# Nine chunks of an RWKV layer on one core: new hand-written orders for all five engines

## What is computed

```
xn = ln(x, ln1);  sx = token_shift(xn)              # previous token minus this one
xxx = tanh((xn + sx*maa_x) @ maa_w1)                # five small mixes
x5 = xn + sx * (maa_stack + xxx @ maa_w2)           # five mixed inputs: k, w, v, r, g
w = exp(-exp(time_decay + tanh(x5[1] @ decay_w1) @ decay_w2))
r, k, v = x5[3] @ Wr.T, x5[0] @ Wk.T, x5[2] @ Wv.T;  g = silu(x5[4] @ Wg.T)
state s (8x8 per head, 32 heads), for each token t:
    a = k_t (x) v_t;  out_t = r_t . (u*a + s);  s = a + w_t * s
x = x + (groupnorm(out) * g) @ Wo.T
xn2 = ln(x, ln2); xr, xk = two mixes of xn2 and its token shift
x = x + sigmoid(xr @ ffn_Wr.T) * (relu(xk @ ffn_Wk.T)**2 @ ffn_Wv.T)
```

## Time and profile before

| | |
|---|---|
| runs | 520.23, 521.76, 522.25 us |
| profiled execution, first to last instruction | 520.3 us |
| VectorE busy | 474.4 us (91%), 528 instructions |
| TensorE busy | 479.2 us (92%) |
| ScalarE busy | 281.7 us (54%) |
| GpSimd busy | 101.6 us (20%) |
| DMA | 69.49 MB, mean 134 GB/s |

### The profile page before, as it was taken

The page is one execution under the profiler, slowest core; times in us unless marked ns, Lnnn a source line. Parts: engine busy times, 40 slices in busy tenths (PEclk is TensorE's granted clock), DMA queues, the critical chain, the costliest instruction groups (busy, mean ns, idle before and its releaser), DMA issues. The chain is left out here.

```text
span 520.3 us, 6254 instructions
## 1 busy us (share of the span) xinstructions
PE 479.2 (92%) x2200; PEld 284.2 (55%) x2200; DVE 474.4 (91%) x528; ACT 281.7 (54%) x612; POOL 101.6 (20%) x93
## 2 busy tenths in 40 slices
...
GB/s 265 121 231 52 107 166 85 145 217 151 72 204 230 122 26 167 220 217 19 103 219 242 85 81 139 216 201 1 121 189 220 78 61 227 126 72 71 1 41 30
DMA packets 26999, 69.49 MB, mean 134 GB/s; under 512 B 1624, under 2 KB 19928, under 8 KB 24536
## 3 DMA queue, kind: packets, MB, share of 16 engines
...
HBM read 46.28 MB, written 12.19 MB: 112 GB/s over the span
## 5 line engine op out<-in xcount | busy, mean ns | idle before, releaser
L630 DVE TENSOR_TENSOR_SCAN kv<-w_sb,kv 128x512 f32<-128x512 f32 (+2 forms) x144 | 146.6, 1084 | 0.1
L958 PE MATMUL pa<-x,large_sb 128*128 128x512 f32 (+2 forms) x272 | 115.2, 567 | 5.0 <-DVE x L545 2.9
L451 POOL COPY kv<-s_sb 128x32 f32<-128x32 f32 (+2 forms) x36 | 54.6, 1518 | 145.6 <-PE patt L1130 141.4
L958 PEld LDWEIGHTS pa<-x,large_sb 128*128 128x128 f32 x272 | 51.2, 194 | 57.5 <-issue 44.3
L620 DVE TENSOR_TENSOR kv<-vrep,k_sb 128x2016 f32<-128x2016 f32 (+2 forms) x34 | 70.1, 2064 | 3.3 <-issue 3.3
L638 DVE TENSOR_TENSOR kv<-kv,r_sb 128x2048 f32<-128x2048 f32 (+2 forms) x36 | 72.9, 2043 | 0.2
L536 DVE SCALAR_TENSOR_TENSOR x<-pb,vec_sb,sx 128x512 f32<-128x512 f32 (+1 forms) x64 | 42.7, 708 | 6.0 <-PE pb L1002 5.9
L420 POOL DMA_DIRECT2D x<-xn x21 | 20.0, 951 | 111.5 <-DVE x L536 111.5
L1130 PE MATMUL patt<-kv,const_sb 128*32 128x512 f32 (+2 forms) x288 | 34.7, 557 | 0.5 <-DVE kv L638 0.4
L1002 PE MATMUL pb<-th,w_sb 32*128 32x512 f32 (+2 forms) x100 | 33.3, 596 | 1.5 <-DVE x L536 1.5
L1156 PE MATMUL pc<-large_sb,att 128*128 128x256 f32 x120 | 32.0, 390 | 0.0
...
## 6 DMA issues: line engine op xcount, KB each, us to landing
...
x<-xn POOLq DMA_DIRECT2D x18, 512.0 KB, 8.3
...
x_tok<-in_x SPq DMA_DIRECT2D x6, 512.0 KB, 10.2
...
xres<-in_x SPq DMA_DIRECT2D x6, 512.0 KB, 10.7
out<-xres SPq DMA_DIRECT2D x6, 512.0 KB, 5.0
out<-trr POOLq DMA_DIRECT2D x6, 512.0 KB, 8.1
```

What stands on the lines that cost most here:

```text
L451: pool.tensor_copy(kv[:, q % 2, :, 0:nb, 0], s0_sb[:, half, G4 * j:G4 * (j + 1), FIRST[c]:FIRST[c] + nb]).then_inc(s0_put, 1)
L630: ins = dve.tensor_tensor_scan(flat, w_sb[:, p, q % HF, 0:nb].rearrange("p b t -> p (b t)"), flat, 0.0, ALU.mult, ALU.add)
L958: ins = pe.matmul(dst[:, m, 0:n], w(a)[:, m * P:(m + 1) * P], src[:, a, :], start=(a == 0), stop=(a == HF - 1))
```

## The change

The lists of head, table and tail are replaced by one list of steps for each engine, over all nine chunks. Every step of before is there once, none is added; instructions, buffers, transfers and `WARM` are the same. One wait is added: `vl1` now waits for the stored v itself, as `vl0` does, since in chunk 0 it comes first.

```
-def schedule(head, table, tail):
+def schedule(text):
+    return [(name, int(c)) for name, c in (step.split(".") for step in text.split())]
...
             def load_v(c, p, half):
-                if half == 0:
-                    sp.wait_ge(v_stored, 16 * JH * (c + 1))
+                sp.wait_ge(v_stored, 16 * JH * (c + 1))
```

The orders, before (-, as the lists unfold) and after (+), in the stretches that are spoken of below. VectorE, start, around `gate` of chunks 3 and 4, and end:

```
-st1.0 nrm1.0 shift.0 mix2.0 mix0.0 cwv.0 mix1.0 mix3.0 cs0.0 a0.0 a1.0 rk.0 shift.1 mix4.0 bonus.0 sc0.0 sc1.0 rs0.0 rs1.0
- mix0.1 a2.0 mix1.1 mix2.1 mix3.1 sc2.0 mix4.1 rs2.0 a3.0 sc3.0 rs3.0 rk.1 a0.1 shift.2 bonus.1 sc0.1 gate.0 mix0.2
+st1.0 nrm1.0 shift.0 cwv.0 mix0.0 mix2.0 mix1.0 mix3.0 cs0.0 a0.0 a1.0 sc0.0 mix4.0 shift.1 rk.0 rs0.0 sc1.0
+ bonus.0 mix0.1 mix1.1 rs1.0 a2.0 mix2.1 sc2.0 mix3.1 rs2.0 a3.0 mix4.1 sc3.0 rs3.0 rk.1 a0.1 bonus.1 shift.2 sc0.1 gate.0 a1.1 mix0.2
...
-rk.3 out.1 a0.3 shift.4 bonus.3 sc0.3 gate.2 rs0.3 mix0.4 mix1.4 a1.3 mix2.4 sc1.3 mix3.4 rs1.3 a2.3
+rk.3 out.1 a0.3 bonus.3 shift.4 a1.3 gate.2 mix0.4 mix1.4 sc0.3 mix2.4 sc1.3 mix3.4 rs0.3 rs1.3 shift2.2 a2.3
-rk.4 out.2 a0.4 shift.5 bonus.4 sc0.4 gate.3 rs0.4 mix0.5
+rk.4 out.2 a0.4 shift.5 bonus.4 gate.3 sc0.4 mix0.5 mix1.5 rs0.4
...
-sc2.7 a3.7 mix4.8 sc3.7 rs2.7 rs3.7 rk.8 out.6 a0.8 a1.8 bonus.8 gate.7 sc0.8 rs0.8 sc1.8 a2.8 sc2.8 rs1.8 rs2.8 shift2.7 a3.8 sc3.8 rs3.8 gate.8 out.7
+a3.7 sc2.7 sc3.7 rs2.7 rs3.7 mix4.8 out.6 a0.8 rk.8 a1.8 gate.7 bonus.8 sc0.8 rs0.8 sc1.8 rs1.8 a2.8 sc2.8 shift2.7 a3.8 sc3.8 rs2.8 rs3.8 out.7 gate.8
```

TensorE, start and end:

```
-T1.0 W1.0 X01.0 X2.0 X3.0 D1.0 D2.0 P0.0 P1.0 VS.0 P3.0 T1.1 CB.0 X4.0 P4.0 BO.0 W1.1 X01.1 S0.0 S1.0 P0.1
+T1.0 W1.0 X01.0 X2.0 X3.0 P0.0 D1.0 P1.0 VS.0 D2.0 T1.1 X4.0 P3.0 P4.0 W1.1 CB.0 X01.1 BO.0 S0.0 P0.1
...
-S2.7 S3.7 CB.8 VR.7 P4.8 WO.7 BO.8 S0.8 T2.7 S1.8 RR.7 S2.8 KK.7 S3.8 VR.8 Y2.7 WO.8
+S2.7 S3.7 VR.7 D2.8 P4.8 CB.8 WO.7 BO.8 S0.8 T2.7 S1.8 RR.7 KK.7 S2.8 S3.8 VR.8 Y2.7 WO.8
```

ScalarE, start and end; SyncE, start and chunk 4:

```
-st.0 nrm.0 xn.0 th.0 thd.0 st.1 v.0 w.0 nrm.1 k.0 r.0 xn.1 tg.0 th.1
+nrm.0 xn.0 st.0 th.0 st.1 thd.0 v.0 k.0 nrm.1 w.0 xn.1 r.0 tg.0 th.1
...
-rr.7 sq.8 kk.7 rstd.8
+rr.7 kk.7 sq.8 rstd.8
-vst.0 lx.0 lr.0 lx.1 lx.2 lx.3 vl0.0 vl1.0 vst.1 vl0.1 vl1.1 sx2.0 lx.4 vst.2 lr.1 vl0.2 vl1.2
+lx.0 lr.0 vst.0 lx.1 vl1.0 vl0.0 lx.2 vst.1 lx.3 vl0.1 vl1.1 sx2.0 vst.2 vl0.2 vl1.2 lr.1 lx.4
...
-vst.4 lr.3 lx.6 vl0.4 vl1.4
+vst.4 sx2.2 vl0.4 lx.6 lx.7 lr.3 vl1.4
```

More of the change, by code:

```diff
@@ L32 @@
 NQ = JH * HF
[L35 to L46, removed]
-SUBS = 3
[L48 to L64, removed]
[6 rows of a table removed]
-            ("out", 0), ("shift", 3), ("bonus", 2), ("sc0", 2), ("gate", 1), ("rs0", 2), ("mix0", 3),
-            ("mix1", 3)]
@@ L73 @@
-PE_HEAD = [("T1", 0), ("W1", 0), ("X01", 0), ("X2", 0), ("X3", 0), ("D1", 0), ("D2", 0), ("P0", 0), ("P1", 0),
[6 rows of a table removed]
-ACT_HEAD = [("st", 0), ("nrm", 0), ("xn", 0), ("th", 0), ("thd", 0), ("st", 1), ("v", 0), ("w", 0), ("nrm", 1),
[5 rows of a table removed]
-POOL_HEAD = [("ad4", 0), ("ad0", 0), ("rd1", 0), ("rd1", 1), ("ad1", 0), ("s00", 0), ("s01", 0), ("ad3", 0),
[3 rows of a table removed]
-SP_HEAD = [("vst", 0), ("lx", 0), ("lr", 0), ("lx", 1), ("lx", 2), ("lx", 3), ("vl0", 0), ("vl1", 0),
-           ("vst", 1), ("vl0", 1), ("vl1", 1), ("sx2", 0), ("lx", 4), ("vst", 2), ("lr", 1)]
+SUBS = 3
```

65 lines of the change are left out of this document (57 added, 8 removed), and 20 rows, old and new, of tables (ACT_HEAD, DVE_HEAD, PE_HEAD, POOL_HEAD).

## The result

The changed kernel takes 531.61 us, the median of 4 runs (529.32, 530.56, 532.66 and 537.10); the kernel before took 522.00 beside it (4 runs, 520.23 to 522.60). The ratio, which is made from the runs side by side and not from the two medians, is 1.0203, 95% interval 1.0146 to 1.0260 (by the medians 1.0184). The forecast was 516.7 us with a range to 522.0: the sign was wrong, and the time lies outside the range.

The account below looks back on a forecast made before the run. VectorE and TensorE were taken as full in the middle, VectorE's free time at the two ends. Start 2.9, chunk 2 2.7, middle -1.0 and end 0.5 sum to 5.1 us off the median: 516.7 us, range 511.0 to 522.0.

Parts of the forecast that it names:

- Nothing can be won in the middle, only lost.: Middle of the kernel: VectorE and TensorE both full, so a new order can win nothing there and only lose.
- Start, chunk 0.: Kernel start: cwv in VectorE's first gap, X4.0 and mix0.1 sooner, less 0.5 us for lx.3; 2.9 us gained.
- The rival in which the clock stays up: Start: TensorE's granted clock does not fall, so the start gives 7.6 us; 512.0 us in all, chance 0.2.
- Chunk 2, +2.7.: Chunk 2: store of v lands 4 us sooner with lx.4 and lr.1 behind the load, ending a0.2's wait; 2.7 us gained.
- The bound of 0: Chunk 2: lower bound of the gain, 0, if GpSimd's accumulating DMAs are what slowed the store of v.
- The rule of the Trainium skill that I weighed at the start: Start: descriptors of one queue go in ring order, so lx.3 delays vl0.1; by it alone 1.0 to 1.7 us gained.
- Middle, +1.0 us of loss.: Chunks 3 to 7: most swaps harmless, gate.3 waits in chunk 4, vl1.4 later; 1.0 us lost, bounds 0 and 4.5.
- The wait of 2.0 us before `gate.3`: Chunk 4: VectorE stands 2.0 us because gate.3 now comes before sc0.4, unless TensorE has got ahead.
- End, +0.5.: Kernel end: kk.7 ahead of sq.8 lets Y2.7 start sooner; 0.5 us gained, bounds -1.5 and 2.
- The slower rival.: Full chunks: mixes one product later make TensorE the bound, four chunks by 2.25 us; 525.7 us, chance 0.12.
- the gain is taken back: Middle costs 4.5 us, or v's store is not sooner or lx.3 costs 2; about 520.5 us, chance 0.22.
- The range.: Whole kernel: 511.0 to 522.0 us, leaving out the slower case, with about 0.17 chance outside.

Follow-up runs that it names:

- head_new: The kernel before with the new order in chunks 0 and 1 alone, its own from chunk 2 on: 519.61 us, ratio 0.9949.
- sp_of_after: The kernel before with the changed kernel's order of SyncE alone: 529.20 us, ratio 1.0071.
- middle_new: x2_store_early with before's order in chunk 2, so everything new except chunk 2: 523.33 us, ratio 0.9990.
- x2_store_early: The changed kernel with sx2.1 to sx2.4 moved ahead of vst.3 to vst.6 on SyncE: 526.19 us, ratio 1.0064.
- hold_v2: x2_store_early with the v load of chunk 2 held back until that chunk's accumulating add is issued: 527.00 us, ratio 1.0099.
- chunk2_new: head_new with the changed orders kept on through chunk 2 (GpSimd's not), sx2.1 early, then before's orders: 524.48 us, ratio 1.0020.
- mix4_back: x2_store_early with mix4 of chunks 2, 5, 7 and 8 put back one product sooner on VectorE: 526.01 us, ratio 1.0074.
- mix4_late: The kernel before with mix4 of chunks 3 to 7 three products later on VectorE: 533.14 us, ratio 1.0215.
- head_tail: head_new with the new order at the very end as well: 519.82 us, ratio 0.9957.

## Why the prediction was wrong, point by point

**"Nothing can be won in the middle, only lost."** Right in its direction, and the loss was then sized far too small. The sentence after it, that VectorE's free time lies at the two ends, was read off one stretch of 20 us: 10.3 of the 45.9 us lay between 60 and 480 us.

*Start, chunk 0.* The steps came as walked, some of them about 1 us late. `mix0.0` stood 4.39 us where it had stood 6.07, since `cwv` is now in the gap, but it also started 0.8 us later than before; the mixes were over at 23.6 (forecast 22.7), and `P0.0` started at 19.89 (18.8). `X4.0` started at 30.18 (forecast 29.3), the granted clock was at 0.50 between 32.5 and 37.5 us and back at 1.00 from 40 on (forecast about 30 to 40), `mix0.1` came at 43.39 (forecast 44.0). That it made up the lateness is partly luck: the clock rose while `P4.0` ran, which was over at 39.0 (forecast 39.7).

```profile
30.00:32.50 2.50, 2.32 (x15) 2.32 (x16) 1.70 (x3) 0.13 (x1) 0.00 (x0) 0.73 1.07 265
32.50:35.00 2.50, 2.50 (x8) 2.08 (x8) 1.94 (x5) 0.00 (x0) 0.00 (x0) 0.50 1.00 220
35.00:37.50 2.50, 2.50 (x7) 2.02 (x6) 2.05 (x4) 0.94 (x2) 0.00 (x0) 0.50 1.01 223
```

`a0.1` started 3.1 us ahead of before, forecast 2.9. `lx.3` in front of the load cost 0.9 us (load issued 7.57 us after the store of v, before 6.64), where 0.5 was taken and 0 to 2 allowed. Taken alone the start was worth 2.3 us at the end (head_new). The rival in which the clock stays up fell.

*Chunk 2, +2.7.* `a0.2` lost its gap, but two steps behind this term failed. The first is the cause of the gain. I wrote that with `lx.4` and `lr.1` behind the load the store of v lands 4 us sooner and the load follows the store by less than 7 us. It followed by 8.7 in after, and SyncE's new list by itself changed nothing (sp_of_after: 10.96 us and a gap of 2.70, before 10.94 and 2.72). The bound of 0 that the prediction gave, for the case that GpSimd's adds are what slowed the store, is what the removal of the two transfers was worth; the 2.2 us came with the new compute orders, so that the gap went is partly luck.

The second step wasn't in the text. I followed the store, the load and `a0.2` but not what the load is ahead of. The load overtook the add of chunk 2, which had been issued 0.9 us ahead of it, and the add's landing went from 5.6 to 20.4 us. I did name the accumulating DMAs, but only as something that might slow the store, never as something that the store's load slows. The trace of before had the price: its adds for `P4` took 5.6 and 5.4 us in chunks 2 and 7, where they were issued ahead of the load, and 18.2 to 20.5 in chunks 3 to 6, behind it. By ratios chunk 2 cost 0.7%, about 3.9 us, where +2.7 was forecast. That the orders of chunk 2 cost this is shown (middle_new against x2_store_early). That they cost it by the wait of `P4.2` is not: hold_v2 and chunk2_new do not have that wait and lost as much, each with a wait on VectorE in its place (7.26 and 6.21 us). So the overtaken add is what stood in after, and what the orders of chunk 2 cost without it stays open.

The rule of the Trainium skill that I weighed at the start was about one queue. The same section of the Trainium skill ("DMA: Bandwidth & Descriptors", "Queues, rings and completion order") also says that each DMA engine goes round-robin between the queues that it has work for, a packet at a time. By it, and if a turn moves as much for either queue, a 0.5 MB add on GpSimd's queue beside a load of 4 MB on SyncE's should get about every second turn and land in some 11 us, twice the 5.6 (an estimate). The trace does not agree for the adds of chunk 2 that are issued behind the load: 20.4 us in after, 20.1 in x2_store_early, 21.1 in mix4_back.

*Middle, +1.0 us of loss.* The wait of 2.0 us before `gate.3` did not come: `gate.3` runs at 247.23 right behind `bonus.4`, its `rstd.3` done at 246.6. `vl1.4`, issued at 237.28 instead of about 228, cost nothing, as said. The new compute orders took exactly before's time from `mix0.3` to `mix0.8` once SyncE was mended (282.5 us). The step that failed is a term put at nothing without a reason. The loss came from the list of SyncE, where the prediction looked at `lr.1`, `lx.4` and `lx.7`, and passed over `sx2`: around chunks 3 to 6 it went from ahead of `vst` to between `vst` and `lr`, which reloads its buffer, twice right ahead of it (`sx2.1`, `sx2.3`). Such a reload waits for the store's whole landing, and so does all that follows in the list. The landing grew as well: 13.5 to 14.9 us for the four stores, before 2.8 to 5.6. The diff showed it, and before, SyncE waited only 0.7 us for `out<-xres`, which was the sign that a cover existed and could be lost. That term alone is 1.4% (5.4 us by the medians), where all moves of SyncE's list in the middle had been put at nothing, at worst 3 us.

*End, +0.5.* The last gap is 6.88 us (forecast near 6) against 7.78. The term was right in size: 0.8 us in every profile with the new end, too little to be told by the times (head_tail against head_new). The way there has the 3.79 us of `bonus.8`. `WO.8` starts 9.3 us after the end of `rs3.8`, before 10.2.

*The slower rival.* Its time, 525.7, was nearer than the forecast, but by luck, since its mechanism isn't what cost the time: undoing what it names in chunks 5, 7 and 8 changed nothing (526.01 against 526.19), and TensorE waited less for VectorE's mixes than before, not more (0.7 us in all for L530, before 3.3 for L536). What is true in it is that the full chunks have almost no slack in the chain mix4, add, P4 (2.2 us a chunk for 6.7 us of delay, mix4_late). The case *the gain is taken back* named the late transfers as its place, with a floor of zero gain; it should have gone on below zero.

*The range.* Every bound of a moved transfer was taken as a wait for the transfer itself, at worst 2 or 3 us. None held what another transfer loses through it, or what an engine's clock adds: `P4.2` waited 5.57 us and then took 3.0 longer at the lower clock. The sum itself is added up rightly, 5.1 us.
